# A fused attention and quantised-FFN kernel: rests of early v and x tiles formed by TensorE and ScalarE, in a new order

## The reference, cut to what matters

```python
def fp4_linear(x, w):
    xq = fp4_quant_dequant(x)
    wq = fp4_quant_dequant(w)
    return jnp.einsum('bsk,nk->bsn', xq, wq)
gate = fp4_linear(x, w_gate)
y = fp4_linear(x, w_up)
h = jax.nn.silu(gate) * y
return fp4_linear(h, w_down)
```

## Time and profile before

| what | value |
|---|---|
| median of 3 runs | 326.03 us (325.96 to 326.42) |
| the profiled execution | 325.95 us, its span 324.1 us |
| granted TensorE clock, mean | 0.998 of full speed |
| PE busy | 313.5 us, 2061 products |
| DVE busy | 293.3 us, 753 instructions |
| ACT busy | 210.2 us, 515 instructions |
| POOL busy | 242.0 us, 258 instructions |

### The profile page before, as it was taken

One profiled execution on the slowest core, in us unless ns is written; L12 is line 12 of the kernel. 1 busy time (PEld: TensorE's weight loads), 2 busy tenths in 40 slices (PEclk: granted clock), 3 DMA queues, 4 the chain that ended last, 5 costly groups with the idle time before them and its releaser, 6 DMA issues.

```text
span 324.1 us, 6506 instructions
## 1 busy us (share of the span) xinstructions
PE 313.5 (97%) x2061; PEld 284.2 (88%) x2061; DVE 293.3 (91%) x753; ACT 210.2 (65%) x515; POOL 242.0 (75%) x258
## 2 busy tenths in 40 slices
PE   8989999999999999999999999999999999999993
PEld 3979888979988999899999999999989889999983
DVE  4989898999898989698996989999999999999982
ACT  7458977594915786348926687467657745666774
...
DMA packets 8241, 15.68 MB, mean 48 GB/s; under 512 B 1040, under 2 KB 5136, under 8 KB 8208
## 3 DMA queue, kind: packets, MB, share of 16 engines
...
...
## 4 chain that ended last, share of the span: by engine, by line
PE 73%; DVE 14%; issue 5%; ACT 4%; POOL 2%; ACTq 0%; DVEq 0%
PE gu L1703 11%; PE gu L1707 11%; PE gu L1704 11%; PE bank L1703 6%; PE bank L1707 5%; PE bank L1704 5%; PE bank L1791 4%; PE bank L1713 3%; PE bank L1717 3%; PE bank L1716 3%; DVE h_y L1075 2%; PE bank L1765 2%; DVE w_raw L1186 2%; PE gu L1716 2%; PE gu L1717 1%
## 5 line engine op out<-in xcount | busy, mean ns | idle before, releaser
L412 POOL TENSOR_TENSOR h_q<-h_g,h_ns 128x704 f32<-128x704 f32 x32 | 47.3, 1478 | 39.2 <-DVE h_g L1080 35.8
L1703 PE MATMUL gu<-guT_hi,xqT_hi 128*128 128x512 f32 (+1 forms) x192 | 74.8, 389 | 0.5 <-DVE w_raw L1186 0.5
L1704 PE MATMUL gu<-guT_lo,xqT_hi 128*128 128x512 f32 (+1 forms) x192 | 72.0, 375 | 0.0
L686 ACT ACTIVATE w_raw<-gu 128x512 f32<-128x512 f32 x64 | 29.3, 461 | 47.2 <-PE gu L1707 46.9
L1707 PE MATMUL gu<-guT_hi,xqT_lo 128*128 128x512 f32 (+1 forms) x192 | 56.7, 376 | 0.5 <-DVE xqT_lo L1177 0.5
L405 POOL TENSOR_TENSOR h_n<-w_raw,h_rs 128x704 f32<-128x704 f32 x32 | 49.0, 1532 | 9.5 <-DVE h_rs L1070 8.9
L1703 PEld LDWEIGHTS gu<-guT_hi,xqT_hi 128*128 128x128 f32 x192 | 36.1, 188 | 6.7 <-issue 1.3
L1707 PEld LDWEIGHTS gu<-guT_hi,xqT_lo 128*128 128x128 f32 x192 | 35.5, 188 | 6.7 <-DVE xqT_lo L1177 0.9
L1704 PEld LDWEIGHTS gu<-guT_lo,xqT_hi 128*128 128x128 f32 x192 | 36.1, 188 | 5.2
L1075 DVE SCALAR_TENSOR_TENSOR h_y<-h_sq,h_n 128x704 f32<-128x704 bf16 x34 | 36.3, 1069 | 1.7 <-ACT h_sq L690 1.7
L1186 DVE TENSOR_TENSOR w_raw<-w_raw,gu 128x512 f32<-128x512 f32 x64 | 32.2, 505 | 2.9 <-ACT w_raw L686 2.1
...
## 6 DMA issues: line engine op xcount, KB each, us to landing
...
scal<-in_scalars_dram ACTq DMA_DIRECT2D x1, 1.0 KB, 1.7
```

Source lines behind the costliest of these rows:

```text
L412: nc.gpsimd.tensor_tensor(blocks(h_q[:, p, 0:I]), blocks(h_g[:, p, :]), per_block(h_ns[:, p, :], HB), ALU.mult).then_inc(h_quant, 1)
L686: nc.scalar.activation(silu[:, p, part[half]], gate_of[half], ACT.Silu).then_inc(silu_ready, 1)
L1703: nc.tensor.matmul(dst, lh, rh, start=(first and i == 0), stop=False)
L1704: nc.tensor.matmul(dst, lh, rl, start=False, stop=False)
```

## The change

1. `v_rest` of batches 0 and 1 (four calls) becomes `v_subtract` on PE and `v_remainder` on ACT. For this the two halves of `values` form one accumulation group in the bank. Later batches keep `v_rest`.
2. `xq_rest` of batch 0 (two calls) becomes `xq_subtract` and `xq_remainder`, with the four transposes as one group.
3. `scale_comb` and the tile `comb` are gone: `round_comb` scales the bank's contents by alpha while it rounds, and `rest_comb` multiplies and subtracts in one operation. `combine` writes into bank[1] in place of bank[3].
4. h_transpose, down and w_transpose use other banks, and the order of the steps is another on every engine.

```diff
-        comb = sb("comb", [P, DK * D])
...
-        h_bank = ((bank[1], bank[0]), (bank[1], bank[0]), (bank[2], gu[:, 3, :]), (bank[3], gu[:, 3, :]))
-        d_bank = (bank[3], bank[0], bank[2], gu[:, 3, :])
-        w_bank = (gu[:, 3, :], bank[0], bank[3], gu[:, 2, :], gu[:, 1, :], gu[:, 0, :], gu[:, 3, :], bank[3], bank[2])
+        h_bank = ((bank[1], bank[0]), (bank[1], bank[0]), (bank[2], bank[3]), (bank[0], bank[2]))
+        d_bank = (bank[2], gu[:, 3, :], bank[3], gu[:, 3, :])
+        w_bank = (bank[0], gu[:, 3, :], bank[3], gu[:, 2, :], gu[:, 1, :], gu[:, 0, :], bank[2], gu[:, 3, :], bank[3])
...
             def round_comb():
-                act.wait_ge(comb_ready, 1)
-                nc.scalar.copy(comb_hi[:].rearrange("p c d -> p (c d)"), comb[:]).then_inc(comb_hi_ready, 1)
+                act.wait_ge(comb_filled, 1)
+                act.wait_ge(act_consts, 2)
+                nc.scalar.activation(comb_hi[:].rearrange("p c d -> p (c d)"), bank[1][:, 0:DK * D], ACT.Copy,
+                                     scale=scal[:, 3:4]).then_inc(comb_hi_ready, 1)
...
+            def v_remainder(n, u):
+                act.wait_ge(v_left, 2 * n + u + 1)
+                c = slice(2 * u, 2 * u + 2)
+                nc.scalar.copy(v_lo[:, c, :].rearrange("p i d -> p (i d)"), v_bank[u][:]).then_inc(v_lo_ready, 1)
...
+            def xq_remainder(n, u):
+                act.wait_ge(xq_left, 2 * n + u + 1)
+                c = slice(D * u, D * (u + 1))
+                nc.scalar.copy(xqT_lo[:, :, c], xq_bank[u][:].rearrange("p (c t) -> p c t", c=DK)).then_inc(xqT_lo_ready, 1)
...
             def v_rest(n, u):
                 dve.wait_ge(v_hi_ready, 2 * n + u + 1)
+                if n == 2 and u == 0:
+                    dve.wait_ge(v_lo_ready, 4)
...
             def xq_rest(n, u):
                 dve.wait_ge(xqT_hi_ready, 2 * n + u + 1)
+                if n == 1 and u == 0:
+                    dve.wait_ge(xqT_lo_ready, 2)
...
-            def scale_comb():
-                dve.wait_ge(comb_filled, 1)
-                dve.wait_ge(act_consts, 2)
-                nc.vector.tensor_scalar(comb[:], bank[3][:, 0:DK * D], scal[:, 3:4], None,
-                                        ALU.mult).then_inc(comb_ready, 1)
             def rest_comb():
                 dve.wait_ge(comb_hi_ready, 1)
-                nc.vector.tensor_tensor(comb_lo[:].rearrange("p c d -> p (c d)"), comb[:],
-                                        comb_hi[:].rearrange("p c d -> p (c d)").bitcast(F32),
-                                        ALU.subtract).then_inc(comb_lo_ready, 1)
+                nc.vector.scalar_tensor_tensor(comb_lo[:].rearrange("p c d -> p (c d)"), bank[1][:, 0:DK * D], scal[:, 3:4],
+                                               comb_hi[:].rearrange("p c d -> p (c d)").bitcast(F32), ALU.mult,
+                                               ALU.subtract).then_inc(comb_lo_ready, 1)
...
+            def v_subtract(n, u):
+                c = slice(2 * u, 2 * u + 2)
+                pe.wait_ge(v_hi_ready, 2 * n + u + 1)
+                nc.tensor.matmul(v_bank[u][:], neg_ident[:], v_hi[:, c, :].rearrange("p i d -> p (i d)"), start=False,
+                                 stop=True, skip_group_check=True).then_inc(v_left, 1)
...
+            def xq_subtract(n, u):
+                c = slice(D * u, D * (u + 1))
+                pe.wait_ge(xqT_hi_ready, 2 * n + u + 1)
+                nc.tensor.matmul(xq_bank[u][:], neg_ident[:], xqT_hi[:, :, c], start=False, stop=True,
+                                 skip_group_check=True).then_inc(xq_left, 1)
...
             scores(0, 1, [])
-            scores(0, 2, [(comb_ready, 1)])
-            scores(0, 3, [(pr_ready, 1)])
+            scores(0, 2, [])
             pe.wait_ge(comb_lo_ready, 1)
             values(0, 0, [])
-            values(0, 1, [])
+            values(0, 1, [(comb_lo_ready, 1)])
+            v_subtract(0, 0)
+            scores(0, 3, [(pr_ready, 1)])
+            v_subtract(0, 1)
             reads(0, 0, [(v_lo_ready, 1)])
+            reads(0, 1, [(v_lo_ready, 2)])
             scores(1, 0, [(pr_ready, 4)])
             scores(1, 1, [(pr_ready, 2)])
-            reads(0, 1, [(v_lo_ready, 2)])
```

More of the change, by code:

```diff
@@ new lines, in _ @@
+            x_squares(1, 1)
+            gate_silu(4, 0, 1)
+            w_remainder(8)
+            x_squares(2, 0)
+            h_repeat(1, 1)
+            x_deviations(2, 1)
+            gate_silu(5, 1, 0)
+            gate_silu(5, 1, 1)
+            h_round(1, 1, 1)
+            x_round(4, 0)
+            xq_round(1, 1)
+            h_repeat(2, 0)
+            h_round(2, 2, 0)
+            p_round(3, 2)
+            out_deviations(0, 0)
+            x_round(4, 1)
+            h_squares(3, 1)
@@ L1878, in _ @@
             values(2, 1, [(xqT_lo_ready, 1)])
-            scores(2, 2, [(wT_lo_ready, 3)])
             gate_up(0, 0, 0, 1)
             gate_up(1, 0, 1, 0)
-            scores(2, 3, [(pr_ready, 9)])
             xq_transpose(0, 1, [(pr_ready, 11)])
             gate_up(1, 0, 1, 1)
+            scores(3, 0, [(pr_ready, 12)])
+            xq_subtract(0, 1)
+            scores(3, 1, [(pr_ready, 10)])
+            reads(2, 0, [(v_lo_ready, 5)])
             gate_up(2, 0, 2, 0)
+            scores(3, 2, [(xqT_lo_ready, 2)])
@@ L1915, in _ @@
-            h_transpose(2, 2, 1, [(pr_ready, 16)])
-            values(3, 1, [(hT_lo_ready, 3)])
-            pe.wait_ge(xqT_lo_ready, 4)
+            pe.wait_ge(wT_lo_ready, 9)
             def body(b):
                 k, n = b * 4, b + 1
+                down(k - 8, 0, [(v_lo_ready, 2 * n + 1)])
+                gate_up(k - 3, b - 1, 1, 1)
+                values(n, 1, [(hT_lo_ready, 8 * n - 21)])
+                xq_transpose(n - 2, 1, [(pr_ready, 4 * n + 3)])
+                h_transpose(k - 6, 2, 0, [(o_ready, k - 7)])
+                down(k - 7, 1, [(pr_ready, k + 8)])
@@ L1944, in body @@
-                scores(n + 1, 3, [(o_ready, 4 * n - 8)])
                 h_transpose(k - 3, 1, 1, [(hT_lo_ready, 2 * k - 6)])
-                gate_up(k + 1, b, 1, 1)
-                values(n + 1, 1, [(hT_lo_ready, 8 * n - 13)])
-                down(k - 4, 0, [(xqT_lo_ready, 2 * n)])
-                h_transpose(k - 2, 2, 0, [(v_lo_ready, 2 * n + 3)])
-                h_transpose(k - 2, 2, 1, [(pr_ready, k + 12)])
-            run(body)
+            run(body)
+            down(12, 0, [(v_lo_ready, 13)])
@@ L1966, in _ @@
             h_transpose(16, 0, 0, [(z_ready, 14)])
[L1967 removed]
+            values(7, 0, [(hT_lo_ready, 32)])
+            h_transpose(16, 0, 1, [(pr_ready, 30)])
+            down(15, 3, [(pr_ready, 29)])
             xq_transpose(5, 0, [(hT_lo_ready, 33)])
[L1969 to L1970 removed]
+            down(16, 0, [(v_lo_ready, 15)])
             gate_up(20, 5, 0, 0)
[L1972 removed]
+            scores(7, 3, [(o_ready, 16)])
```

1268 lines of the change are left out of this document (626 added, 642 removed).

## The result

The changed kernel takes **324.36 us** (median of 5 runs, 324.26 to 324.63) beside 326.02 for the kernel before (325.96 to 326.42); the ratio is 0.9939, its 95% interval 0.9922 to 0.9956. The forecast was 324.4. Its profiled execution took 324.26 us with a span of 322.5, against 325.95 and 324.1: 1.6 us of span to account for.

What follows compares the result with a forecast made beforehand. The prediction took PE's stream of products, with a few holes, as the bound. From 325.95 us, -1.1, -0.3 and -0.2 gave 324.35; with 0.08 for the median of the runs, 324.4 us, range 322.9 to 326.9.

Steps and rivals of the forecast that it cites:

- 1 to 4, up to gate_up(0): From the start to the first gate_up: -1.1 us together, bounds -2.1 and +0.4, gate_up(0) starting at 39.98.
- 8, the end: Tile 27's transposes follow the last gate_up, so the last tiles' chain starts earlier: -0.2 us, bounds -0.6 and +0.4.
- Term 1: Six added PE products of 512 columns, 0.23 us each: +1.4 us of PE, bounds 0 and 2.4.
- Term 2: Before about 55 us, 4.2 us of operations leave DVE; ACT takes six copies, +3.0 us.
- Term 3: Start, walked in the new order: the 1.1 us hole goes; scores(1,1) ends at 21.85, 1.1 us gained.
- Term 4: On to the first gate_up: only xq_subtract(0,0) waits, 0.25 us; gate_up(0) starts at 39.98.
- Term 5: 40 to 110 us: two waits behind a stretched h_y, DVE further ahead now; -0.3 us, bounds -0.8 and +1.5.
- Term 6: The loop, 110 to 200 us: PE's own work per batch unchanged, nothing to gain; 0.
- The second rival: Loop holes where stretched DVE operations delay hidden before gate_up of tile 3: 5 x 0.6 = 3.0 us, 327.4 us, chance 0.14.
- Term 7: 200 to 270 us, DVE nearly full: new order, same load; 0, bounds -0.8 and +1.0.
- The first rival: Gain isn't kept: DVE, nearly full from 60 to 110 and 200 to 270 us, sets the pace; 325.9 us, chance 0.15.

Runs made afterwards that it cites:

- run 9: Changed kernel with six added products of zeros in the loop (batches 2 to 4), where PE has no idle time: 325.05 us, ratio 0.9968.
- run 1: Changed kernel with the four v rests of batches 0 and 1 back on DVE: 325.93 us, ratio 0.9955.
- the ballast: Seven idle DVE operations of 512 columns, results unread, put into the changed kernel between 13 and 50 us: 326.58 us.
- runs 3 and 4: Changed kernel with seven idle DVE operations put in (326.58 us, ratio 0.9998), and with only the last three of them (324.76 us, ratio 0.9962).
- run 2: Kernel before with one line moved, reads(0,1) ahead of scores(1,0) and scores(1,1): 329.76 us, ratio 1.0082.
- Run 3: Changed kernel with seven idle DVE operations put in, whose result nobody reads: 326.58 us, ratio 0.9998.
- run 10: Changed kernel with down(13) ahead of gate_up(18), just behind the loop: 323.55 us, ratio 0.9917.

## Why the prediction was right, and where it wasn't

The total was right to 0.1 us, but by luck in part, since errors of 0.5 to 0.8 us in four of the five rows cancel. Per term:

| term | forecast | measured |
|---|---|---|
| 1 to 4, up to gate_up(0) | -1.1 | -0.6 |
| 5, 40 to 110 | -0.3 | -1.1 |
| 6, 110 to 200 | 0 | +0.7 |
| 7, 200 to 270 | 0 | -0.7 |
| 8, the end | -0.2 | -0.15 |

The first is gate_up(0) at 40.52 against 39.95 with the same 1.37 less 0.23 us ahead of it; the others are the changes of PE's idle time. They sum to -1.85, the span changed by -1.6; the rest is in distances that no wait names.

- *Term 1, six products at 1.4.* Their own distance is right (0.22 in run 9), the net cost isn't: six more cost 0.5 us beside them and 0.7 in the loop. The Trainium skill, Perfetto Trace Analysis, section Identifying the Most-Contended Engine, takes the share of the weight loads, 88% here, as the measure of TensorE's headroom. By it six products would fit into the 12% left. The runs stand between: each takes its 0.22 us where it is issued, and half or more comes back from lateness further on. And run 1 shows a hole of 1.6 us where the four of v stood.
- *Term 2, DVE relieved.* Work on DVE counts for the first two batches only: at their four places the ballast costs 1.8 us, and behind them 0.4 (runs 3 and 4). But with the real rests there, and their four products gone, it was 0.2 where the clock held (run 1), so how much of the gain is DVE's relief stays open between these two.
- *Term 3, the walk of the start.* Right at each mark to 0.15 us. The order without the faster rests loses 0.8% (run 2).
- *Term 4.* This is the term that was most off at the start: gate_up(0) came 0.54 us late. Of it 0.34 is one wait for ACT that the walk didn't have: the wait of 0.25 us before xq_subtract(0,0) was foreseen (40.19), a like one before w_subtract(0) at 26.9 wasn't: the two v_subtracts start at 26.57 and w_subtract at 27.37, where two distances of 0.23 would give 27.03 (ACT's copy of the weights, 0.58 us from 26.73, ends at 27.31). The other 0.2 isn't traced.
- *Term 5.* The text looked for the cause of the two waits in DVE's load and in a stretched h_y. Run 3 has the old load and no holes, so it was the order. The two xqT_lo that PE had waited for, at 68.93 and 101.31, on DVE's timeline before and in the changed kernel:

```profile
68.20 0.67 DVE L1177 TENSOR_TENSOR xqT_lo<-bank,xqT_hi 128x512 fp32r<-128x512 f32 x1
...
99.36 1.15 DVE L1148 TENSOR_SCALAR z_nm<-z_sum 128x2 f32<-128x2 f32 x1 [1.15 <-ACT z_off L666]
...
100.49 0.68 DVE L1177 TENSOR_TENSOR xqT_lo<-bank,xqT_hi 128x512 fp32r<-128x512 f32 x1
```

```profile
67.02 0.69 DVE L1200 TENSOR_TENSOR xqT_lo<-bank,xqT_hi 128x512 fp32r<-128x512 f32 x1
...
97.28 0.69 DVE L1200 TENSOR_TENSOR xqT_lo<-bank,xqT_hi 128x512 fp32r<-128x512 f32 x1
```

  The second never had the cause that the forecast gave: ahead of 100.49 DVE was idle for 1.15 us, waiting for ACT, and no stretched h_y stood there. The step that failed is "the new order pairs DVE and POOL anew" taken as zero.
- *Term 6.* The second rival, a hidden value late behind a stretched DVE operation, happened once (0.58 us), behind the loop, and in no turn of it; where `down` stands between, as in run 10, it is covered. Its price for one hole (0.6) was right, its place and its count weren't.
- *Term 7.* Three waits of before (0.37 at 212.3, 0.18 at 235.8, 0.33 at 263.5, for pr and w_raw) went with the new order; no run separates them.
- *The first rival* (gain given back where DVE is full) is out: behind 40 us PE's idle time is 6.3 us in all where it was 7.6, with DVE at 66 of 70 us from 200 to 270.

What the change brings, undone piece by piece in the new order: the quantised x 1.2 us (at the place tried), the combined weights 0.9, v's rests 0.2 (1.6 where the clock falls). They sum to more than the 1.66 us that the change gains; each is worth what it is worth only with the others in place. That the order is worth nothing without them is shown for one line of it (run 2), not for the whole.
